# Down-weight scaling ahead of the first hidden tile, and an earlier order of loads before the second attention

## What is computed

```python
x = x + jnp.tanh(g_xattn[0]) * _L0_xattn_ref(_layernorm(x), ctx_2048, ...)   # FP8-rounded projections, 16 heads of 128
x = x + jnp.tanh(g_ffn[0])   * _L0_ffn_ref(_layernorm(x), gate_w, up_w, down_w, gate_s, up_s, down_s)
x = x + jnp.tanh(g_xattn[1]) * _L1_xattn_ref(_layernorm(x), ctx_2048, ctx_2048, mask, w_q, w_k, w_v, w_o, b_o)
x = x + jnp.tanh(g_ffn[1])   * _L1_ffn_ref(_layernorm(x), w_gate, w1, w2)    # 8 experts, top 1, capacity 256

# _L0_ffn_ref
g = jnp.einsum('th,ih->ti', xf, gate_w) * gate_s          # inner width 704
u = jnp.einsum('th,ih->ti', xf, up_w) * up_s
out = jnp.einsum('ti,hi->th', jax.nn.silu(g) * u, down_w) * down_s

# _L1_xattn_ref: 32 heads of width 8 in 8 groups, causal and padded
scores = jnp.einsum('bnghd,bmgd->bnghm', q, k) / scale    # then the masks and a softmax
out = jnp.einsum('bnghm,bmgd->bnghd', attn, v).reshape(B, S, D) @ w_o.T + b_o
```

## Time and profile before

| what | value |
|---|---|
| median of 3 runs | 1454.85 us (1449.39 to 1459.92) |
| the profiled execution | 1459.92 us, of which the traced span is 1457.6 us |
| TensorE busy / VectorE busy | 1349.2 / 1150.8 us |
| ScalarE busy / GpSimd busy | 985.6 / 809.1 us |
| mean granted clock of TensorE | 0.975 |

### The profile page before, as it was taken

One profiled execution on the slowest core, in us unless ns is written; L12 is line 12 of the kernel. 1 busy time (PEld: TensorE's weight loads), 2 busy tenths in 40 slices (PEclk: granted clock), 3 DMA queues, 4 the chain that ended last, 5 costly groups with the idle time before them and its releaser, 6 DMA issues.

```text
span 1457.6 us, 29426 instructions
## 1 busy us (share of the span) xinstructions
PE 1349.2 (93%) x11260; PEld 1149.4 (79%) x11260; DVE 1150.8 (79%) x2271; ACT 985.6 (68%) x2174; POOL 809.1 (56%) x794
## 2 busy tenths in 40 slices
PE   1677999999999999999999999799998999996898
PEld 1567999999999999999999998667763455555898
DVE  8999889888888889888889889763357686877464
ACT  5896877887878787878787777531215555573675
POOL 5677556656566566556566444310005676773675
PEclk9899999999999999999999999999998999997899
DMA  3200000100100100100001000045532430106462
GB/s 110 58 9 30 19 20 16 33 6 16 37 2 16 38 10 7 38 15 12 27 16 49 7 2 16 12 135 59 79 68 59 59 67 2 45 2 214 170 237 97
DMA packets 59979, 69.75 MB, mean 48 GB/s; under 512 B 6811, under 2 KB 52091, under 8 KB 59712
## 3 DMA queue, kind: packets, MB, share of 16 engines
q1 hardware_dynamic: 56720, 58.64, 16.1%
q0 software_dynamic: 2944, 9.19, 1.8%
q10 hardware_dynamic: 176, 0.04, 0.0%
HBM read 55.56 MB, written 12.34 MB: 47 GB/s over the span
## 4 chain that ended last, share of the span: by engine, by line
PE 70%; DVE 15%; POOL 6%; issue 3%; DMA 3%; SPq 2%; ACT 1%; POOLq 0%; DVEq 0%; ACTq 0%
PE PC L453 7%; PE SS L419 6%; PE PO L435 5%; PE PA L387 4%; PE B L399 4%; PE PA L364 3%; PE B L1079 3%; PE PA L366 3%; PE B L1570 3%; PE PO L1063 2%; DVE QN L700 2%; POOL WR L816 2%; PE SS L2094 2%; PE PA L1521 2%; PE B L2094 2%
## 5 line engine op out<-in xcount | busy, mean ns | idle before, releaser
L873 POOL TENSOR_TENSOR RB<-YS,M 128x512 bf16<-128x512 f32 x128 | 162.9, 1273 | 256.0 <-DVE YS L726 256.0
L548 ACT ACTIVATE QT<-B,sm 128x256 f32<-128x256 f32 x256 | 131.3, 565 | 166.6 <-PE B L399 166.6
L419 PE MATMUL SS<-QT,KT 128*128 128x256 f32 x512 | 156.0, 399 | 10.5 <-DVE mx L681 10.2
L364 PE MATMUL PA<-WH,XQ 128*128 128x256 f32 x512 | 141.6, 308 | 19.6 <-POOL XQ L804 14.8
L869 POOL TENSOR_TENSOR yy<-vv,half 128x12 f32<-128x12 f32 x64 | 147.3, 2302 | 5.3
L366 PE MATMUL PA<-WL,XQ 128*128 128x256 f32 x512 | 130.7, 287 | 0.0
L1695 ACT ACTIVATE P<-PO,mcf 128x1024 f32<-128x1024 f32 x64 | 71.4, 1115 | 81.7 <-PE PO L1555 81.7
L700 DVE TENSOR_TENSOR QN<-QN,yy 128x512 f32<-128x512 f32 x128 | 123.6, 966 | 1.9 <-POOL yy L869 1.9
L681 DVE TENSOR_REDUCE mx<-SS 128x4 bf16<-128x512 f32 x128 | 88.0, 687 | 44.2 <-PE SS L411 44.2
L693 DVE TENSOR_REDUCE vv<-SQ 128x6 f32<-128x768 f32 x128 | 120.5, 941 | 0.3 <-ACT SQ L580 0.3
L364 PEld LDWEIGHTS PA<-WH,XQ 128*128 128x128 f32 x512 | 99.2, 194 | 20.6 <-issue 15.2
(11 more groups left out here) (349 smaller groups left out, 4360.2 us busy)
## 6 DMA issues: line engine op xcount, KB each, us to landing
W<-in_w SPq DMA_DIRECT2D x16, 1024.0 KB, 6.5
Q<-qsc SPq DMA_DIRECT2D x48, 128.0 KB
WR<-in_wprojT SPq DMA_DIRECT2D x16, 256.0 KB, 3.0
K<-ksc SPq DMA_DIRECT2D x12, 256.0 KB
qsc<-T POOLq DMA_DIRECT2D x8, 384.0 KB, 3.0
X<-in_x SPq DMA_DIRECT2D x4, 512.0 KB, 7.5
CR<-in_xctxT SPq DMA_DIRECT2D x8, 256.0 KB, 2.9
RSM<-rsm_d SPq DMA_DIRECT2D x16, 128.0 KB, 4.1
```

What stands on the lines that cost most here:

```text
L364: pe.matmul(PA[:, 256 * k:256 * k + 256], XQ[:, k, c, bs], wh[:, c, 256 * k:256 * k + 256], start=c == 0, stop=False)
L419: pe.matmul(SS[:, 256 * z:256 * z + 256], k[:, 128 * z:128 * z + 128], q[:, 256 * z:256 * z + 256], start=True, stop=False)
L548: a.activation(QT[i % 2][:, o:o + 256], B1[:, o:o + 256], ACT.Identity, bias=col(n + "b"), scale=col(n + "w"))
L873: p.tensor_tensor(RB[i % 2][:], YS[:], M[:], ALU.subtract).then_inc(s_rb, 1)
```

## The change

The scaling of the down weights moves on VectorE from behind tile 4 of quad 0 to the front of the feed forward's loop, ahead of the first hidden tile. In attention 1 the query loads of quads 2 and 3 move from behind the maxima of blocks 2 to 5 to behind the maxima of blocks 0 to 3. The loads of `WO` and `WG` move from SP's step 14 to its step 12, ahead of the maxima of block 2. `OTS` is allocated ahead of `AO`, so that it and the tiles after it have other addresses; with that, the first copy into `OTS` waits for the query stores of quads 2 and 3 instead of the last parts being made (`s_ql`), and the first `dve_normalise` drops its wait for the stores of quad 3. No instruction that computes is added or removed.

SP's order after the change: queries of quads 0 and 1, maxima 0, first half of quad 2 (after its stores), maxima 1, second half of quad 2, `WO` and `WG` (after the stores of quad 3), maxima 2, first half of quad 3, maxima 3, second half of quad 3, maxima 4 and so on.

```diff
--- before.py
+++ after.py
@@ -1271,13 +1271,6 @@
             v.wait_ge(s_ka, 2 * q4 + 2)
             v.tensor_tensor(ks[:, 2, :], RK, ks[:, 1, :], ALU.subtract).then_inc(s_kl, 1)
 
-        def dve_down_weights(v):
-            v.wait_ge(s_fd, 48)
-            v.tensor_scalar(DS[:], DS[:], th[:, 2:3], None, ALU.mult).then_inc(*vs.up())
-            v.wait_ge(*vs.at())
-            v.tensor_tensor(DW[:, 0:5, :], DW[:, 0:5, :], DS[:].unsqueeze(1).broadcast_to([128, 5, H]), ALU.mult)
-            v.tensor_tensor(DW[0:64, 5, :], DW[0:64, 5, :], DS[0:64, :], ALU.mult).then_inc(s_dw, 1)
-
         def dve_mask_row(v):
             v.wait_ge(s_row, 48)
             v.tensor_copy(mrf, mrow).then_inc(*vs.up())
@@ -1319,13 +1312,16 @@
             dve_parts(v, 0)
             after_attention_0(v)
             dve_parts(v, 2)
+            v.wait_ge(s_fd, 48)
+            v.tensor_scalar(DS[:], DS[:], th[:, 2:3], None, ALU.mult).then_inc(*vs.up())
+            v.wait_ge(*vs.at())
+            v.tensor_tensor(DW[:, 0:5, :], DW[:, 0:5, :], DS[:].unsqueeze(1).broadcast_to([128, 5, H]), ALU.mult)
+            v.tensor_tensor(DW[0:64, 5, :], DW[0:64, 5, :], DS[0:64, :], ALU.mult).then_inc(s_dw, 1)
             for q4 in range(4):
                 for n in range(NI):
                     dve_hidden(v, q4, n)
                     if q4 == 0 and n < 4:
                         dve_keys_values(v, n)
-                    if q4 == 0 and n == 4:
-                        dve_down_weights(v)
                     if q4 == 0 and n == 2:
                         dve_mask_row(v)
                     if q4 == 0 and n == 3:
@@ -1388,13 +1384,13 @@
         WO = sb("WO", [128, 2, H])
         VE = [sb(f"VE{i}", [128, 4, 128], FR) for i in range(2)]
         VO0 = sb("VO0", [128, 4, 128])
+        OTS = [sb(f"OTS{i}", [128, 512]) for i in range(2)]
         AO = [sb(f"AO{i}", [128, H]) for i in range(2)]
         AOT = sb("AOT", [128, 2, 128])
         rl = sb("rl", [128, 4, 4])
         low = sb("low", [128, 4, 2, 8])
         WG = sb("WG", [128, 2, E])
         fill0 = sb("fill0", [128, 672])
-        OTS = [sb(f"OTS{i}", [128, 512]) for i in range(2)]
         PH1 = [sb(f"PE1{i}", [128, 2, 256], FR) for i in range(3)]
         PL1 = [sb(f"PL1{i}", [128, 2, 256], FR) for i in range(3)]
         P1 = [sb(f"P1{i}", [128, 1024]) for i in range(4)]
@@ -1493,9 +1489,9 @@
                 b = every(n, 4, 5, NB)
                 if b is not None:
                     sp_maxima(sp, b)
-                    if 2 <= b < 6:
-                        sp_queries(sp, 1 + b // 2, b % 2)
-                if n == 14:
+                    if b < 4:
+                        sp_queries(sp, 2 + b // 2, b % 2)
+                if n == 12:
                     sp.wait_ge(s_down, 16)
                     sp.wait_ge(s_qst[3], 32)
                     sp.dma_start(WO[:], w1o.rearrange("(c p) n -> p c n", p=128)).then_inc(s_wog, 16)
@@ -1703,7 +1699,8 @@
         def act_evac_out(a, u):
             a.wait_ge(s_LO, N + 2 * u + 2)
             if u == 0:
-                a.wait_ge(s_ql, 8)
+                a.wait_ge(s_qst[2], 32)
+                a.wait_ge(s_qst[3], 32)
             if u >= 2:
                 a.wait_ge(s_T2, N + u - 1)
             a.activation(OTS[u % 2][:], OT[u % 2][:], ACT.Copy).then_inc(s_rt, 1)
@@ -1771,8 +1768,6 @@
             b, hb = divmod(u, 2)
             t4 = TR[u % 2][:].rearrange("p (j g c) -> p j g c", g=4, c=32)
             v.wait_ge(s_T2, N + u + 1)
-            if u == 0:
-                v.wait_ge(s_qst[3], 32)
             v.tensor_copy(low[:], t4[:, :, ::2, 9:17]).then_inc(*vs.up())
             v.reciprocal(rl[:], t4[:, :, :, 8])
             v.wait_ge(*vs.at())
```

## The result

| kernel | median of 8 runs (us) | profiled execution (us) |
|---|---|---|
| before | 1454.19 (1449.39 to 1459.92) | 1459.92 |
| after | 1465.85 (1461.45 to 1471.88) | 1467.68, span 1465.5 |

The ratio is 1.0076, with a 95% interval of 1.0047 to 1.0104: the change makes the kernel slower by 11.7 us by the medians (7 to 15 us by the interval). The forecast was 1456 us in a range of 1448 to 1464, so the measured time lies above the range; the loss is about ten times the 1.2 us of its sum.

What follows compares the result with a forecast made beforehand. TensorE, busy 93% of the span, was taken as the bound, so only its waits and slow clock count. The terms +4.9 - 5.4 + 1.7 + 0 gave +1.2 us, a median of 1456 us, range 1448 to 1464.

Steps and rivals of the forecast that it cites:

- Part 1: Feed forward: early scaling waits for DS and delays TensorE's second keys and values step; idleness plus slow clock, +4.9 us.
- The term of the idleness: Feed forward: TensorE idle 2.6 us before its second keys and values step, able to begin at 957.3 instead of 954.66.
- Part 2: Attention 1: WG lands before the first output projection, so its wait and the slow clock behind it go, -5.4 us.
- the 3.3 us: Attention 1: share of the WG wait's 5.4 us put down to slow clock, beside 2.1 us of idleness.
- Part 3: Attention 1: moved query batches delay maxima behind them in the rings; 1.0 us waiting plus 0.7 clock, +1.7 us.
- a wait at step 12: Attention 1, shifted scores: TensorE waiting there was named as a sign that the forecast falls; no size given.
- The margin of 1.1 us at step 12: Attention 1: maxima of block 1 land about 1114, before their reader, the shifted scores, starts at 1115.15.
- up to 2 us more beside a batch: Attention 1: query stores sharing engines with a query batch might take about 2 us more to land.
- Part 4: Attention 1: OTS's new address and moved waits add no instruction and cost 0 us.
- ScalarE's 2.12 us of idleness: Attention 1: ScalarE's idle time before its exponential at 1124.41 hides the later first copy into OTS.
- step 16 that is late: Attention 1: maxima of block 2 reach their reader 0.4 us late, up to 2.5 us with slow stores.
- Rival (b): Attention 1: ring order makes block 2's maxima late at step 16; +6.3 us in all, 1461 us, chance 0.20.

Runs made afterwards that it cites:

- a1: The kernel before with only the scaling of the down weights moved ahead of the first hidden tile; 1460.88 us against 1453.55, ratio 1.0043.
- b4: The kernel before with the scaling of the down weights behind tile 1 of quad 0 instead of tile 4; 1454.37 us against 1453.33, ratio 1.0004.
- c1: The kernel before with the first half of quad 2's queries loaded behind WO and WG instead of ahead; 1451.34 us against 1453.87, ratio 0.9982.
- d1: The kernel before with the four query batches of quads 2 and 3 each one block later; 1450.05 us against 1453.39, ratio 0.9978.
- a2: The changed kernel with the scaling put back behind tile 4; 1458.65 us, ratio 1.0025 against before.
- b3: The changed kernel with quad 2's second half behind maxima 2 and quad 3's halves behind maxima 3 and 4; 1461.93 us, ratio 1.0045 against before.
- a4: The kernel before with only the query loads of quads 2 and 3 moved two blocks ahead; 1462.59 us, ratio 1.0062.
- b2: The changed kernel with OTS and its waits as before the change; 1465.04 us, ratio 1.0081 against before.
- b1: The kernel before with only OTS in its new place and the waits that go with it; 1452.29 us against 1453.33, ratio 0.9994.
- c2: The kernel before with the scaling at the front and the DW and DS loads issued ahead of the context's second quarter; 1459.72 us against 1453.87, ratio 1.0039.

## Why the prediction was wrong

**Part 1, the scaling (forecast +4.9, bounds 2.6 to 5.9).** The mechanism was right in each step: wait for DS, hidden tile, RK, value copy, second keys and values step, slow clock behind, nothing given back. The size was too small: 6.3 us measured in a1 (3.6 to 8.9), above the upper bound of 5.9. The term of the idleness was mis-sized: 2.6 us forecast, 4.95 in the kernel after and 4.4 to 5.1 in three more of the five executions. DS took 6.6 us instead of 5.7, and TensorE arrived at 953.4 instead of 954.66, since it ran the first gate products at full clock. That taking the work away from tile 4 gains nothing is what b4 fits.

**Part 2, WG (forecast -5.4).** About twice too much, and this was the first step that failed. The wait and its cause were right: WG lands in 2.5 us once no batch is ahead, and the projection does not wait. Its price was not. The distance of 17.91 us between two turns in one execution was taken as what the wait costs. In four more executions with the same wait it was 14.9 to 17.35, and in three of them no slow clock stood behind the wait, so the 3.3 us of it were what one execution paid, not what the wait costs each time. The mean of the five is 3.6 us. c1 and d1 agree: with the wait gone the kernel gains 2.6 us (and a wait of 1.27 us stands elsewhere) and 3.2 us. What decides whether the clock falls is open.

**Part 3, the queries (forecast +1.7, bounds 0 to 5.8).** The second step that failed, by the most. From the +3.6 of a2 and a gain of 2.6 to 3.2 at WG, parts 3 and 4 together cost 6 to 7 us; this is what is left over, no run measures it alone. The prediction had named a wait at step 12 as a sign that the forecast falls, and it came, 3.09 us long. Two things went wrong. The margin of 1.1 us at step 12 was worked out as batch (11.7 us) plus about 0.9 for the maxima. In b3, with one batch ahead and none behind, DMA activity ended 12.9 us after the batch's issue and the reader went on 15.0 us after it (1122.22 - 1107.25); in the kernel after, with a second batch behind them, it was 16.5 us (1123.88 - 1107.40). a2, a4 and b2 have the second batch too and took 15.1, 16.4 and 16.8 us. So the reader goes on 2.4 to 4.2 us later than computed, and most of that is there with one batch alone; that the second batch adds to it is not shown. And the stores of quad 3 were given up to 2 us more beside a batch; the copy behind them began 9.2 us after their issue.

**Part 4, OTS (forecast 0).** Right by itself (b1). The sentence that ScalarE's 2.12 us of idleness hide the wait, or that it lies inside the bound of part 3 if they don't, was too light: the copy stands in front of the exponential, so late stores stop the whole pipeline there. Before, the copy began 2.2 us after the first of these stores was issued (1121.72 - 1119.53), in the kernel after 9.2: 7.0 us more, of which the 2.12 us of cover leave 4.9, the 4.84 us that TensorE is idle. The slow clock behind it, 0.53 for 6 us, is worth about another 3 us in this execution (an estimate: half of the 6 us). In the prediction it is step 16 that is late by 0.4 to 2.5 us; in the trace there is no wait at step 16 at all; TensorE had stopped at steps 12 and 14 before.

Rival (b), the other side, had the mechanism that decided: transfers behind the batches in the rings. Its place was wrong (maxima of block 2 at step 16, where it was those of block 1 and the stores), and its price of +6.3 us in all too low, chiefly because it kept the gain of 5.4. The runs' own sum is 6.3 (a1) + 3.6 (a2) = 9.9 us, against 11.0 by the ratio. The Trainium skill, page "DMA: Bandwidth & Descriptors", section "Queues, rings and completion order", names the order within a ring and that an increment comes only after the engine's earlier writes; the trace agrees (4 KB in 11.6 us). The section "Issuing engines are not separate DMA queues" of the same page says that DMAs of GpSimd and SP run on the same engines and interleave, which the prediction did not price from any row. The runs agree: 6.3 us with a batch beside them, 3.3 without.

## What to carry to other kernels

Before loads are moved earlier in a queue, list every small transfer and every store that will then find them ahead or beside, with its deadline; a load that nobody waits for gains nothing by being early, and here the better kernel sends it later, one batch to a block. Work that needs a load goes behind it in an in-order engine's stream, not in front of what feeds the bottleneck: the same 2.13 us with their wait cost 6.3 us at the front and nothing behind tile 1. And what a wait costs should not be read as the distance between two marks in one execution: the slow clock behind one and the same wait was worth anything from nothing to 3.3 us in five executions, so take several, or remove the wait and measure.

## What the runs showed of the hardware

The same wait of TensorE of 2.1 to 2.9 us, at the same place and behind nearly the same work, was followed by 6.8 us at a granted clock of 0.53 in the profiled execution of before, by 3.75 us at 0.54 in c2, and by no slow clock in a1, b1 and b4. The waits of 2.5 to 5.1 us in the feed forward were followed by slow key matmuls (3.42 to 3.65 us instead of 1.93) in all five executions that have them.

Six loads of 128 KB each, to 8 partitions each, kept 0.55 to 0.6 of the DMA engines' time busy for 11.7 us (before) and 12.9 us (b3); a row of 4 KB issued behind them took up to 11.6 us although nearly half of the engines' time was free, against 1.7 us for the rows of maxima that before sent between 1104 and 1110 with no batch ahead. Two stores of 384 KB from GpSimd took 3.3 us without a batch of SP's beside them (before, b3) and 6.3 us with one (after, a4, b2; 5.4 in a2).

Two DMAs that share a semaphore are best read as a pair: the view gives 2.3 us for the first of the two rows of maxima of block 1 in the kernel after, and 11.6 us for the second, and TensorE, which waits for both, went on with the second.
